# Linear attention: the product with the running state in four column parts, turned afterwards

## The reference, cut to what matters

```python
b, n, c = x.shape                                   # 8, 512, 128; 16 heads of 8 columns
qkv = (x @ qkv_w.T).reshape(b, n, 3, H, HD).transpose(2, 0, 3, 1, 4)
q, k, v = (qkv[0], qkv[1], qkv[2])
phi_q = relu(q) + EPS
phi_k = relu(k) + EPS
kv = einsum('bhnd,bhne->bhnde', phi_k, v)
S = cumsum(kv, axis=2)                              # one 8 x 8 state per head, summed over tokens
out = einsum('bhnd,bhnde->bhne', phi_q, S)
out = out / maximum(scale * pos, EPS)
out = out.transpose(0, 2, 1, 3).reshape(b, n, c)
return out @ proj_w.T
```

## Time and profile before

| | |
|---|---|
| median of 3 runs | 713.81 us (713.1 to 714.46) |
| profiled execution | 715.88 us |
| its span, first to last instruction | 713.9 us |
| mean granted TensorE clock | 0.981 of full speed |
| PE / DVE / ACT / POOL busy | 647.1 / 587.4 / 455.0 / 307.9 us |
| first `states` to second `up` of the second mixture | 147.4 to 270.9 us |

### The profile page before, as it was taken

One profiled execution on the slowest core, in us unless ns is written; L12 is line 12 of the kernel. 1 busy time (PEld: TensorE's weight loads), 2 busy tenths in 40 slices (PEclk: granted clock), 3 DMA queues, 4 the chain that ended last, 5 costly groups with the idle time before them and its releaser, 6 DMA issues. The chain is left out here.

```text
span 713.9 us, 15983 instructions
## 1 busy us (share of the span) xinstructions
PE 647.1 (91%) x5778; PEld 465.5 (65%) x5778; DVE 587.4 (82%) x1538; ACT 455.0 (64%) x865; POOL 307.9 (43%) x417
## 2 busy tenths in 40 slices
PE   4999999978999989999999699898898987899895
PEld 2777777657888876777777356565565755556564
DVE  3788889855667579988889899999799998999983
ACT  3777779666655616777788567667656535666742
POOL 5000002145565432000013476754977675677520
PEclk9999999989999999999999799999999999999998
DMA  8100000000000000000000000000000000010000
GB/s 215 23 0 0 0 0 1 2 2 3 3 2 0 3 4 0 1 1 1 0 1 1 0 1 1 0 1 1 0 1 2 1 1 1 0 30 16 29 16 29
DMA packets 13464, 7.07 MB, mean 10 GB/s; under 512 B 1304, under 2 KB 13408, under 8 KB 13408
## 3 DMA queue, kind: packets, MB, share of 16 engines
q1 hardware_dynamic: 11328, 5.27, 2.8%
q10 hardware_dynamic: 2080, 1.05, 0.5%
HBM read 4.22 MB, written 2.10 MB: 9 GB/s over the span
## 5 line engine op out<-in xcount | busy, mean ns | idle before, releaser
L1510 PEld LDWEIGHTS ps<-expert_work 128*128 128x128 f32 x1024 | 132.0, 192 | 70.5 <-ACT expert_work L632 50.5
L1133 DVE SCALAR_TENSOR_TENSOR x_sb<-ps,gates,x_sb 128x128 f32 (+1 forms) x512 | 143.4, 343 | 34.1 <-PE ps L1510 26.9
L1510 PE MATMUL ps<-expert_work 128*128 128x128 f32 x1024 | 138.1, 278 | 2.6 <-ACT expert_work L632 2.5
L1510 PE MATMUL ps<-xnT,expert_work 128*128 128x512 f32 x256 | 134.1, 607 | 0.0
L366 POOL TENSOR_SCALAR vareps<-meanvar 128x4 f32<-128x4 f32 (+1 forms) x28 | 8.9, 319 | 237.2 <-DVE meanvar L1047 236.6
L628 ACT ACTIVATE expert_work<-ps 128x512 f32<-128x512 f32 x128 | 75.5, 590 | 54.6 <-PE ps L1510 54.2
L632 ACT ACTIVATE expert_work<-expert_work 128x512 f32<-128x512 f32 x128 | 80.6, 630 | 4.0
L1510 PE MATMUL ps<-gateT,xnT 128*128 128x352 f32 x128 | 56.7, 525 | 14.5 <-ACT ffn_work L763 11.3
L413 POOL TENSOR_TENSOR shared<-shared 128x128 f32<-128x128 f32 x112 | 51.0, 455 | 27.3 <-ACT shared L722 19.1
L1510 PE MATMUL ps<-downT,hqT 128*128 128x128 f32 x384 | 57.3, 288 | 4.2 <-ACT hqT L873 3.9
L606 ACT ACTIVATE xn<-x_sb,shift,rstd 128x128 f32<-128x128 f32 (+1 forms) x136 | 57.1, 481 | 5.0 <-POOL shift L374 5.0
(11 more groups left out here) (174 smaller groups left out, 1329.0 us busy)
## 6 DMA issues: line engine op xcount, KB each, us to landing
x_sb<-in_L_attn_x_dram SPq DMA_DIRECT2D x8, 256.0 KB, 7.1
out_dram<-x_sb SPq DMA_DIRECT2D x8, 256.0 KB, 2.3
expert_work<-in_L_ffn_w_all_dram ACTq DMA_DIRECT2D x2, 512.0 KB, 6.1
wraw<-in_L_attn_qkv_w_dram SPq DMA_DIRECT2D x1, 192.0 KB, 4.9
wraw<-attn_in_proj_weight_dram SPq DMA_DIRECT2D x1, 192.0 KB, 3.8
fraw<-in_L_ffn_w_down_dram SPq DMA_DIRECT2D x1, 176.0 KB, 2.8
fraw<-in_L_ffn_w_gate_dram SPq DMA_DIRECT2D x1, 128.0 KB, 2.1
fraw<-in_L_ffn_w_up_dram SPq DMA_DIRECT2D x1, 128.0 KB, 2.2
```

Source lines behind the costliest of these rows:

```text
L1133: t = nc.vector.scalar_tensor_tensor(tile_b(i, j), bank(4 + e % 4, TPB, C)[:, j, :], gates[:, j, e:e + 1], tile_b(i, j), ALU.mult, ALU.add)
L1510: return nc.tensor.matmul(o, a, b, start=start, stop=stop, **kw)
```

## The change

In the linear attention, `take_states` moves from ScalarE to VectorE, as one product of all 16 states (2048 columns out of PSUM) with the block mask `blockdiag`; what lies between heads is now zero. GpSimd's setting to zero of the buffer goes. `across` uses the queries as weights, 32 columns at a time, in the four column parts of the array, and the state as the moving operand; it fills bank 0 with the result by token, once for a group and not in two halves. ScalarE carries it out (`past_out`), TensorE transposes it (`turn_past`), ScalarE carries it out again (`past_turned_out`), and the first instruction of each `pick` adds it. `phi_k` is made by ScalarE in two instructions in place of one on VectorE. For the first group `q_bd` is made by GpSimd.

At the entry, `values_in` and `turn_keys` of group 0 move into the last group of the first mixture, the layer norms of groups 1 and 2 move earlier there, and ScalarE's instructions with them. In body 7 `router(0, 0)` moves behind `turn_past`, and VectorE's `gating(0)` behind `residual(6)`, ahead of the last `pick`; before it stood ahead of the first. At the start of the kernel each tile is transposed as soon as it is normalised, and `up(0, 0, 0)` goes ahead of `router(0, 0)`.

GpSimd:

```diff
-                pool.wait_ge(s["state_taken"], HQ * i + HQ)
+                pool.wait_ge(s["state_taken"], i + 1)
...
-                    nc.gpsimd.memset(state, 0.0).then_inc(s["state_zero"], 1)
                     ln_group(s, 0, TPB)
                     ln_group(s, 1, TPB)
+                    first_masked_queries(s)
                     ln_group(s, 2, TPB)
```

ScalarE, whose body was `normalise(i+2)`, `front(i+1)`, `take_states(i+1)`, `evac_xnT(i+2)` before; `front` keeps its order, with `keys_out` new at its head:

```diff
+                def keys_out(i):
+
+                    act.wait_ge(s["k_done"], i + 1)
+                    nc.scalar.activation(phi_k[:, :], bank(1, T), ACT.Relu).then_inc(s["phik_ready"], 1)
+                    act.wait_ge(s["phik_ready"], 2 * i + 1)
+                    nc.scalar.activation(phi_k[:, :], phi_k[:, :], ACT.Identity,
+                                         bias=att_eps[:, 0:1]).then_inc(s["phik_ready"], 1)
+
+                def past_out(i):
+
+                    act.wait_ge(s["past_done"], 2 * i + 1)
+                    nc.scalar.activation(past[:, :, :], bank(0, TPB, C), ACT.Copy).then_inc(s["past_ready"], 1)
+
+                def past_turned_out(i):
+                    act.wait_ge(s["past_done"], 2 * i + 2)
+                    nc.scalar.activation(pastT[:, :].rearrange("p (c j n) -> p j c n", c=NCH, j=TPB),
+                                         bank(0, TPB, NCH, CH), ACT.Copy).then_inc(s["past_ready"], 1)
...
                 def body(i, side):
...
+                    if known_below(i, GROUPS - 1):
+                        front(i + 1, 1 - side)
+                    past_out(i)
+                    past_turned_out(i)
                     if known_below(i, GROUPS - 2):
-                        ahead(i + 2)
-                    else:
+                        evac_xnT(s, i + 2)
+                    elif i == GROUPS - 2:
+                        evac_xnT(nxt, 0)
+                    if known_below(i, GROUPS - 3):
+                        act.wait_ge(s["tr_done"], i + 3)
+                        normalise(s, i + 3, TPB, tile_b)
```

VectorE:

```diff
                 def pick(i, half, side):
 
                     dve.wait_ge(s["att_done"], 2 * i + half + 1)
+                    if half == 0:
+                        dve.wait_ge(s["past_ready"], 2 * i + 2)
...
+                def take_states(i, side):
+
+                    dve.wait_ge(s["state_done"], i + 1)
+                    nc.vector.tensor_tensor(state[:, side, :, :, :].rearrange("p c j f -> p (c j) f"),
+                                            ps[:, 2:6, :].rearrange("p c (j f) -> p (c j) f", j=TPB),
+                                            blockdiag[:, :].unsqueeze(1).to_broadcast([P, NCH * TPB, C]),
+                                            ALU.mult).then_inc(s["state_taken"], 1)
+
                 def body(i, side):
                     more = known_below(i, GROUPS - 1)
-                    if more:
-                        keys(s, i + 1)
                     scores(i, 2, side)
                     scores(i, 3, side)
                     if more:
-                        queries(s, i + 1)
+                        queries(s, i + 1, 1 - side)
...
-                    if not more:
-                        gating(0)
+                    if more:
+                        take_states(i + 1, 1 - side)
                     pick(i, 0, side)
                     if not (type(i) is int and i == 0):
                         residual(i - 1)
...
                     if not more:
+                        gating(0)
+                    pick(i, 1, side)
+                    if not more:
                         gating_end(0)
 
                         dve.wait_ge(s_fw, 80)
                         w4.largest()
                         w4.scales()
-                    pick(i, 1, side)
```

TensorE (`keys_in(i)` now waits for `x_done` at `i - 1`, and no longer for the second `pick` of body `i - 2`):

```diff
+                def across(i, side):
+
+                    pe.wait_ge(s["prefix_ready"], (TPB * NCH - 2) * i + TPB * NCH - 2)
+                    for j in range(TPB):
+                        for c in range(NCH):
                             pj, pc = divmod(NCH * j + c - 1, NCH)
-                            t = mm(bank(6 + c % 2, TPB, P)[:, j, :], state[:, side, pj, pc, :],
-                                   q_bd[:, side, :, P * j + CH * c:P * j + CH * c + CH],
-                                   start=False, stop=True, skip_group_check=True)
-                    t.then_inc(s["att_done"], 1)
+                            t = mm(bank(0, TPB, C)[CH * c:CH * c + CH, j, :],
+                                   phi_q[:, side, P * j + CH * c:P * j + CH * c + CH],
+                                   state[:, side, pc, pj, :] if j + c > 0 else no_state[:, :],
+                                   tile_position=(0, CH * c))
+                    t.then_inc(s["past_done"], 1)
+
+                def turn_past(i):
+                    pe.wait_ge(s["past_ready"], 2 * i + 1)
+                    for j in range(TPB):
+                        t = nc.tensor.transpose(bank(0, TPB, P)[:, j, :], past[:, j, :], ident[:, :])
+                    t.then_inc(s["past_done"], 1)
...
                     within(i, 0, side)
                     if more:
                         states(i + 1, 1 - side)
-                    across(i, 0, side)
+
+                        pe.wait_ge(s["reluq_ready"], i + 2)
+                    else:
+                        pe.wait_ge(nxt["xnT_ready"], 1)
+                    across(i, side)
                     if not (type(i) is int and i == 0):
                         project_out(i - 1, 1 - side, more)
-                    if not more:
-                        up(0, 0, 0)
+                    turn_past(i)
                     if more:
-
-                        pe.wait_ge(s["reluq_ready"], i + 2)
+                        scores(i + 1, 1 - side, 0)
+
+                        pe.wait_ge(s["past_ready"], 2 * i + 2)
                         if known_below(i, GROUPS - 2):
                             transposes(s, i + 2)
                         else:
                             transposes(nxt, 0)
-                        scores(i + 1, 1 - side, 0)
-                    within(i, 1, side)
-                    across(i, 1, side)
-                    if more:
                         scores(i + 1, 1 - side, 1)
+                        within(i, 1, side)
                     else:
+                        up(0, 0, 0)
+                        pe.wait_ge(s["past_ready"], 2 * i + 2)
+                        router(0, 0)
+                        within(i, 1, side)
                         up(0, 1, 0)
                         down(0, 0)
```

203 lines of the change are left out of this document (112 added, 91 removed).

## The result

In 20 executions the changed kernel took 710.86 us (median; 706.52 to 716.65), the kernel before 714.51 (20; 712.85 to 715.86): a ratio of 0.9949, with a 95% interval of 0.9927 to 0.9972. The change gains 3.7 us; I had forecast 14. What I did not expect is the spread, 10 us in place of 3. Each execution comes with its mean granted clock, and the time follows it: 706.52 to 707.76 us at 0.978 to 0.981, 714.93 to 716.65 at 0.966 to 0.971.

The account below looks back on a forecast made before the run. The prediction took TensorE to bound the loop (busy 13.72 of 13.93 us a body), and the evacuation chain after the change. Terms -4.0 - 4.7 - 7.3 + 1.0 + 1.0 = -14.0 us took 713.81 to 699.8, range 695.5 to 706.

Parts of the forecast that it names:

- I take it that the clock stays up: First body: TensorE idles 1.9 us, not 2.84, so its clock was assumed to hold, worth about 3.0 us.
- entry, with the start: Scores of group 0 start at 148.0 instead of 152.0: -4.0 us, including 0.8 from earlier transposes at the kernel's start.
- first body: Second `pick` of group 0 at 162.35 instead of 171.09, beyond the earlier entry: -4.7 us.
- six bodies: Loop: 12.9 us a body by the chain through the evacuations, 77.4 us instead of 84.7: -7.3 us.
- exit: From the second `pick` of group 6 to the third expert's `up`: 16.1 us instead of 15.1, +1.0 us.
- VectorE's backlog: VectorE begins the second mixture 2.6 us later, TensorE only 1.0: +1.0 us allowed (0 to 2.6).
- The four banks let it lag: Second mixture: four banks let VectorE run behind TensorE, so only +1.0 us was allowed for its lateness.
- Column parts: `across`: 32 records run side by side in four parts of the array, 1.1 us with the gap instead of 3.5.
- in turn: Rival, `across`: column parts don't overlap with short products, `across` takes 3.5 us, kernel 720.6 us; chance 0.04.
- The loop gains nothing: Rival, loop: hand-overs cost each body 1.2 us more, so the six bodies gain nothing, 707 us; chance 0.17.
- the clock falls: Rival, entry: TensorE's clock falls there after all, 3.3 us more, 703 us; chance 0.15.

Follow-up runs that it names:

- both_busy: Changed kernel plus unused TensorE products at the entry (two of 512 columns, one more in the first body) and exit (four before the last `within`): 704.99 us.
- changed_again: The changed kernel unaltered, timed and profiled a second time as a control: 710.83 us.
- before_entry: Kernel before plus three unused TensorE products of 512 columns ahead of the scores of group 0: 3.5 us slower.
- before_idle: Kernel before, with TensorE made to wait in each body but the first for the previous group's second `pick`: 722.80 us.
- before_ends: Kernel before plus unused products at both ends of the linear attention: five of twelve executions at 710.08 to 710.47 us, six at 715.50 to 721.36.
- entry_busy: Changed kernel plus two unused products before the scores of group 0 and one in the first body: 2.3 us below the changed kernel.

## Why the prediction was wrong, by its own steps

- **The step that failed is "I take it that the clock stays up".** I counted 3.0 of the first body's 4.7 us on it, and priced a fall only at the entry, as a rival with a chance of 0.15. At the exit and in the loop I gave it no price. Between 144 and 290 us the two profiles of the changed kernel lose 8.5 and 6.8 us of clock, the one before 3.4. Outside they lose 6.8 (falls at 399 and 695) and 8.5 (one more at 584), so of the mean of 17.6 some 9 to 11 lie inside: an estimate. At 0.85 us each that is 8 to 9 us. Measured: both_busy, whose only edit is to keep TensorE busy at the ends, lies 4.0 below the changed kernel by the ratios, 4.7 by the means, and still has falls.

The terms, from the same landmarks in the profiles; "clock held" is changed_again up to the last body and both_busy at the exit, where no fall lies:

```
                              forecast   changed   clock held
entry, with the start           -4.0      -3.0       -3.8
first body                      -4.7      -0.8       -4.1
six bodies                      -7.3      -4.4       -5.5
exit                            +1.0      +2.9       +1.2
VectorE's backlog               +1.0      +2.2       +2.2
sum                            -14.0      -3.1      -10.0
rest of the kernel               0        -2.5
```

Even with the clock held the sizes were 4.0 us too good. Against that stand 2.5 us that nobody forecast: behind the second mixture the profile of the kernel before has 10.2 us of clock lost and this one 6.8. No run ties that to the change, and before_entry, before_idle and before_ends, without it, lose 6.8 there too; it is luck, and it hides part of the miss. With it the kernel would stand near 702 to 703 without its falls in the linear attention, which is where the line of 0.85 us puts it too (701.7 to 703.1).

- **Entry, -4.0:** -3.0 in one profile (148.99), -3.8 in the other (148.19). Size right, cause partly wrong: the zeroing had no part that can be seen. The start gave 0.6 of 0.8 (the first `xnT` at 10.32).
- **First body, -4.7:** with the clock up, from the scores to the second `pick` it is 14.96 us (163.15 - 148.19) against 19.09 before: -4.1. The rest is GpSimd: its sums of group 0 end late, and `across` waits 0.82 for them, a wait that I left out. With the falls it is -0.8.
- **Six bodies, -7.3:** measured -4.4, and -5.5 where the clock held (79.2 us from 163.15 to 242.38). The steady body is right to the hundredth, 12.90, with the chain and the wait where I laid them. What I missed: the 14.1 I took for before is an average that holds TensorE's gaps called "issue" at the seam of loop and unrolled code (steady bodies there are 13.93), and the changed kernel keeps them; its last body takes 14.44 in changed_again. I compared an average with a body free of gaps.
- **Exit, +1.0:** +2.9 (18.1 us against 15.2; the 15.1 of the prediction ends at the weight load, 0.11 ahead of `up`). With the clock at 1.00 there, in both_busy, it is 16.4, so +1.2: the layout stands, the 1.2 GHz are the rest.
- **VectorE's backlog, +1.0 (0 to 2.6):** +2.2. From `up` for the third expert to the first product of the feed-forward behind the second mixture it is 122.3 us in all four profiles of the kernel before and its variants, and 124.6 to 124.7 in all sixteen of the changed kernel and its own. "The four banks let it lag" is what failed: TensorE pays nearly all of it. The rows name VectorE's late sums and `ex`, over GpSimd's `shift` and ScalarE. Before, then changed, from their timelines:

```profile
271.04 1.02 PE L1510 MATMUL ps<-xnT,expert_work 128*128 128x512 f32 x2
...
285.90 0.23 ACT L623 ACTIVATE exs<-ex 128x32 f32<-128x32 f32 x1 [0.50 <-DVE ex L1102]
...
393.39 0.76 PE L1510 MATMUL ps<-gateT,xnT 128*128 128x352 f32 x2
```

```profile
270.56 0.88 ACT L638 ACTIVATE xn<-x_sb,shift,rstd 128x128 f32<-128x128 f32 x2 [0.76 <-POOL shift L378]
...
282.70 0.23 ACT L655 ACTIVATE exs<-ex 128x32 f32<-128x32 f32 x1 [1.75 <-DVE ex L1140]
...
284.13 1.16 PE L1563 MATMUL ps<-expert_work 128*128 128x128 f32 x8 [0.97 <-ACT expert_work L664]
...
390.31 0.76 PE L1563 MATMUL ps<-gateT,xnT 128*128 128x352 f32 x2
```

- **Column parts:** 32 records in 1.1 us, as forecast; the rival "in turn" was rightly given little. **The loop gains nothing:** wrong, and rightly at 0.17.
- The rival "the clock falls" was priced too low: one fall at one place, 3.3 us, where there are several, at places that change from one execution to the next.

Open stays what decides when the clock falls. Shown is that the same code with the same idle time falls in one execution and not in the next; that in the kernel before a microsecond idle per body does not do it; that in the changed kernel filling both ends takes 7 us of lost clock away and filling one end 3 to 6; and that where a fall is kept away at one place the profile can have others at later ones (entry_busy, before_entry). The Trainium skill (TensorE: Matmul & The Clock Gate, section A second HAM failure mode: psum-queue depth-cycling) tells of a kernel whose clock swings although its idle stretches are short. The fall of entry_busy at 190 agrees; the loop of before_idle, with longer ones and none, doesn't.

## What to carry to other kernels

When a change takes work off TensorE and leaves a handover chain in its place, forecast the clock with it: give each new idle stretch a fall as the likely case, and look at the spread and the mean clock of all executions, not at one profile. Where idle stretches at the ends of a stage can't be filled with work moved from elsewhere, a few unused products made some 2 to 6 us here; but the kernel before became 3.5 us slower by those at its entry alone, and in the loop, where a chain is the bound, they brought nothing, so measure many executions of each. When work moves to another engine, follow the lag into the next stage: here it cost 2.2 us there in every profile. Before an order is changed to remove a wait, look at what the moved work was covering.

## What the runs showed of the hardware

- TensorE's granted clock fell at 149.7, 166.8 and 248.7 in one execution of a kernel, and at 243.3 and 256.9 in another, with the same 2.01 us of idle time at the entry.
- A granted clock of 0.50 does not double everything: keys and queries go from 1.98 to 3.78 us, 128 records of small scores at most from 2.02 to 3.38, and the span pays 0.85 us for each us of clock lost, since other engines bound part of it.
- A GpSimd zeroing of 3.51 us stretches a VectorE instruction of 0.29 us to 3.28, and no difference is seen in the kernel's time.
- `across` as 16 products (32 records) with 32 columns of weights takes 0.94 us more when doubled, 29 ns a record.
